# Gelu evaluated twice by ScalarE in the FFN of a fused attention + FFN block, VectorE's cast of its values removed

## The reference

```
x = x + attn(layernorm(x))     # layernorm inside attn again; gated, relu^2 linear attention,
                               # 16 heads of 32, causal running sums kv and k, then W_proj
x = x + ffn(layernorm(x))      # P = x@U1 (512->128); H = gelu_tanh(P@V1 + b1) (128->2048)
                               # Q = H@U2 (2048->128); Q@V2 + b2 (128->512)
```

## Time and profile before

| what | value |
|---|---|
| median of 3 runs | 1833.25 us (1833.06 to 1835.95) |
| the profiled execution's own time | 1834.25 us |
| its span in the trace | 1831.9 us |
| PE busy | 1792.6 us, 98% |
| PE weight loads (PEld) | 1539.9 us, 84% |
| DVE busy | 1448.5 us, 79% |
| ACT busy | 683.9 us, 37% |
| POOL busy | 798.7 us, 44% |
| granted PE clock over the span | 0.995 |
| chain that ended last, by engine | PE 93%, DVE 1% |

### The profile page before, as it was taken

How to read it: one execution, slowest core, us unless ns; L and a number is a source line. 1 busy time by engine, 2 the same in 40 slices (tenths; PEclk the granted TensorE clock), 3 DMA queues, 4 the chain that set the end, 5 groups by cost and what they waited for, 6 DMA issues and landing times.

```text
span 1831.9 us, 34348 instructions
## 1 busy us (share of the span) xinstructions
PE 1792.6 (98%) x13753; PEld 1539.9 (84%) x13753; DVE 1448.5 (79%) x2606; ACT 683.9 (37%) x1242; POOL 798.7 (44%) x1027
## 2 busy tenths in 40 slices
PE   7899999999999999999999999999999999999997
PEld 4688888888888888888888888888888888888876
DVE  7777878878878878878878788778887788787775
ACT  4233343343333333333333433333433433333332
POOL 3253444444444444435434444434444444444430
PEclk9999999999999999999999999999999999999999
DMA  6001000001010011010011010011010010100000
GB/s 216 26 13 35 29 31 31 24 29 36 24 35 24 24 36 36 24 36 25 24 36 36 24 36 24 25 35 35 25 36 24 24 36 25 35 24 27 28 18 24
DMA packets 34508, 61.06 MB, mean 33 GB/s; under 512 B 3672, under 2 KB 6256, under 8 KB 34352
## 3 DMA queue, kind: packets, MB, share of 16 engines
q1 hardware_dynamic: 33488, 57.31, 9.6%
q10 hardware_dynamic: 864, 1.57, 0.2%
HBM read 41.96 MB, written 16.91 MB: 32 GB/s over the span
## 4 chain that ended last, share of the span: by engine, by line
PE 93%; DVE 1%; POOL 0%; ACT 0%; issue 0%
PE ps_a L786 9%; PE ps_a L784 9%; PE ps_a L785 9%; PE ps_t L791 6%; PE ps_b L786 6%; PE ps_b L785 6%; PE ps_b L784 6%; PE ps_q L784 4%; PE ps_b L984 3%; PE ps_h L784 3%; PE ps_h L785 3%; PE ps_h L786 3%; PE ps_q L785 3%; PE ps_q L786 3%; PE ps_c L962 3%; PE ps_c L974 3%
## 5 line engine op out<-in xcount | busy, mean ns | idle before, releaser
L378 POOL TENSOR_TENSOR h_lo<-h_full,h_hi 128x512 fp32r<-128x512 f32 x244 | 313.8, 1286 | 500.7 <-DVE h_hi L604 500.7
L459 ACT ACTIVATE h_full<-ps_h,cols 128x256 f32<-128x256 f32 x512 | 211.1, 472 | 243.7 <-PE ps_h L786 236.0
L604 DVE CAST h_hi<-h_full 128x512 fp32r<-128x512 f32 x256 | 176.2, 688 | 98.0 <-ACT h_full L459 97.8
L784 PE MATMUL ps_b<-wx_hi,zt_hi 128*128 128x512 f32 x512 | 206.9, 404 | 5.3 <-DVE key_sums L714 3.1
L784 PE MATMUL ps_a<-wx_hi,zt_hi 128*128 128x512 f32 x512 | 208.2, 407 | 0.0
L786 PE MATMUL ps_b<-wx_hi,zt_lo 128*128 128x512 f32 x512 | 203.3, 397 | 0.0
L785 PE MATMUL ps_b<-wx_lo,zt_hi 128*128 128x512 f32 x512 | 203.2, 397 | 0.0
L786 PE MATMUL ps_a<-wx_hi,zt_lo 128*128 128x512 f32 x512 | 202.3, 395 | 0.0
L785 PE MATMUL ps_a<-wx_lo,zt_hi 128*128 128x512 f32 x512 | 201.8, 394 | 0.0
L340 POOL TENSOR_TENSOR small<-moments,eps_col 128x1 f32<-128x1 f32 x128 | 25.8, 201 | 391.5 <-DVE moments L753 327.1
L784 PE MATMUL ps_q<-h_hi,u_hi 128*128 128x256 f32 x512 | 159.5, 311 | 7.3 <-DVE h_lo L609 5.1
(11 more groups left out here) (173 smaller groups left out, 5053.0 us busy)
## 6 DMA issues: line engine op xcount, KB each, us to landing
xs<-L_attn_x SPq DMA_DIRECT2D x64, 256.0 KB, 2.8
out<-x1s SPq DMA_DIRECT2D x64, 256.0 KB, 2.1
key_sums<-carry_rows SPq DMA_DIRECT2D x60, 256.0 KB, 3.2
x1s<-L_attn_W_gate SPq DMA_DIRECT2D x4, 256.0 KB, 4.0
x1s<-L_ffn_U SPq DMA_DIRECT2D x4, 256.0 KB, 3.8
carry_rows<-key_sums SPq DMA_DIRECT2D x64, 2.0 KB
probs<-L_attn_W_qkv SPq DMA_DIRECT2D x3, 256.0 KB, 6.0
bias<-L_attn_b_qkv ACTq DMA_DIRECT2D x3, 256.0 KB, 6.8
```

The source lines that it names most:

```text
L378: E.tensor_tensor(h_lo[:, i % 2, :], h_full[:, i % 2, :], h_hi[:, i % 2, :].bitcast(F32), ALU.subtract).then_inc(s["h_lo_ready"], 1)
L459: last = E.activation(h_full[:, i % 2, a * GROUP:(a + 1) * GROUP], ps_h[i % 2][:, a * GROUP:(a + 1) * GROUP], ACT.Gelu_apprx_tanh, bias=b1 ...
L604: E.tensor_copy(h_hi[:, i % 2, :], h_full[:, i % 2, :]).then_inc(s["h_hi_ready"], 1)
L784: E.matmul(ps, wh, mh, start=start and i == 0, stop=False)
```

## The change

ScalarE evaluates gelu twice from PSUM for each half of a pair: once into `h_full` (fp32), once into `h_hi` (fp32r). Four ACTIVATEs instead of two, and only the last signals `h_full_ready`. DVE's CAST is gone; POOL's subtraction (and in the last steps DVE's) now waits for ACT. The semaphore `h_hi_ready` is gone.

```diff
             def h_tail(g, i):                                    # POOL
-                pool.wait_ge(s["h_hi_ready"], g.done(PAIRS, i + 1))
+                pool.wait_ge(s["h_full_ready"], g.done(PAIRS, i + 1))
                 E.tensor_tensor(h_lo[:, i % 2, :], h_full[:, i % 2, :], h_hi[:, i % 2, :].bitcast(F32),
                                 ALU.subtract).then_inc(s["h_lo_ready"], 1)
...
             def gelu(g, i):                                      # ACT
                 act.wait_ge(s["h_done"], g.done(PAIRS, i + 1))
-                for a in range(2):
-                    last = E.activation(h_full[:, i % 2, a * GROUP:(a + 1) * GROUP],
-                                        ps_h[i % 2][:, a * GROUP:(a + 1) * GROUP], ACT.Gelu_apprx_tanh,
-                                        bias=b1_cols[:, 2 * i + a:2 * i + a + 1])
+                for out_ in (h_full, h_hi):
+                    for a in range(2):
+                        half = slice(a * GROUP, (a + 1) * GROUP)
+                        last = E.activation(out_[:, i % 2, half], ps_h[i % 2][:, half], ACT.Gelu_apprx_tanh,
+                                            bias=b1_cols[:, 2 * i + a:2 * i + a + 1])
                 last.then_inc(s["h_full_ready"], 1)
...
-            def h_head(g, i, tail=False):                        # DVE
+            def h_tail(g, i):
                 dve.wait_ge(s["h_full_ready"], g.done(PAIRS, i + 1))
-                E.tensor_copy(h_hi[:, i % 2, :], h_full[:, i % 2, :]).then_inc(s["h_hi_ready"], 1)
-                if tail:
-                    dve.wait_ge(s["h_hi_ready"], g.done(PAIRS, i + 1))
-                    dve.wait_ge(s["h_lo_ready"], g.done(PAIRS, i))
-                    E.tensor_tensor(h_lo[:, i % 2, :], ...)
+                dve.wait_ge(s["h_lo_ready"], g.done(PAIRS, i))
+                E.tensor_tensor(h_lo[:, i % 2, :], ...)
...
-                if ffn.exists:                 # five such places: h_head in every step
-                    h_head(ffn, pairs[3], finishing)
+                if ffn.exists and finishing:   # now h_tail in the last steps alone
+                    h_tail(ffn, pairs[3])
```

More of the change, by code:

```diff
@@ L197, in block_kernel @@
             y_done x1_steps x1_small z1_ready x1b_ready tx_done x1t_hi_ready x1t_ready
-            p_done pt_hi_ready pt_ready h_done h_full_ready h_hi_ready h_lo_ready
+            p_done pt_hi_ready pt_ready h_done h_full_ready h_lo_ready
             qacc_done qt_hi_ready qt_ready result_done result_ready carry_in""".split()
@@ L600, in squared_relu @@
                     .then_inc(chain, 1)
-            def h_head(g, i, tail=False):
+            def h_tail(g, i):
                 dve.wait_ge(s["h_full_ready"], g.done(PAIRS, i + 1))
-                E.tensor_copy(h_hi[:, i % 2, :], h_full[:, i % 2, :]).then_inc(s["h_hi_ready"], 1)
-                if tail:
-                    dve.wait_ge(s["h_hi_ready"], g.done(PAIRS, i + 1))
-                    dve.wait_ge(s["h_lo_ready"], g.done(PAIRS, i))
-                    E.tensor_tensor(h_lo[:, i % 2, :], h_full[:, i % 2, :], h_hi[:, i % 2, :].bitcast(F32),
-                                    ALU.subtract).then_inc(s["h_lo_ready"], 1)
+                dve.wait_ge(s["h_lo_ready"], g.done(PAIRS, i))
+                E.tensor_tensor(h_lo[:, i % 2, :], h_full[:, i % 2, :], h_hi[:, i % 2, :].bitcast(F32),
+                                ALU.subtract).then_inc(s["h_lo_ready"], 1)
             def step(p, b):
@@ L665, in step @@
                         .then_inc(s["pt_ready"], 1)
-                if ffn.exists and b % 2 == 0:
-                    h_head(ffn, pairs[0], finishing)
+                if ffn.exists and b % 2 == 0 and finishing:
+                    h_tail(ffn, pairs[0])
                 if n.exists:
@@ L676, in step @@
                     tile_tails(early_tiles)
-                if ffn.exists:
+                if ffn.exists and finishing:
                     if b % 2:
-                        h_head(ffn, pairs[0], finishing)
-                    h_head(ffn, pairs[1], finishing)
+                        h_tail(ffn, pairs[0])
+                    h_tail(ffn, pairs[1])
                 if c.exists:
@@ L687, in step @@
                             .then_inc(s["probs_ready"], 1)
-                    if ffn.exists:
-                        h_head(ffn, pairs[2], finishing)
+                    if ffn.exists and finishing:
+                        h_tail(ffn, pairs[2])
                     dve.wait_ge(s["state_done"], c.done())
@@ L700, in step @@
                         .then_inc(s["ot_ready"], 1)
-                elif ffn.exists:
-                    h_head(ffn, pairs[2], finishing)
+                elif ffn.exists and finishing:
+                    h_tail(ffn, pairs[2])
                 z_tail(Chunk(p, b + 1))
-                if ffn.exists:
-                    h_head(ffn, pairs[3], finishing)
+                if ffn.exists and finishing:
+                    h_tail(ffn, pairs[3])
                 if n.exists:
```

## The result

The changed kernel takes **1846.05 us** (median of 4 runs, 1845.22 to 1848.57) against 1833.38 for the kernel before: ratio **1.0071, 95% interval 1.0058 to 1.0083**. It is 12.7 us slower; I had forecast 18.0 (1851). The profiled execution took 1845.22 us, 11.0 more than the profiled one of before, and the spans differ by 11.2 us. What follows explains these 11; the other 1.7 of the medians is within what single runs differ by (2.9 us between the shortest and the longest run of the kernel before).

A forecast was written before the change was run, and what follows sets the result against it. PE, busy 1648.45 of 1650 us, was taken to be bound by how late its next operand is; 16.2 (30 x 0.54) + 0.5 + 1.3 gave +18.0 us, forecast 1851.2; own range 1847 to 1856, overall range 1836 to 1857.

The forecast's parts named there:

- second rival: Odd step: L721 gets in ahead of h_lo of pair 3, q_pair 3 waits 0.25 us; 11 us slower, 1844; chance 0.08.
- h_lo starts 0.28 later: Each pair where DVE was free for the cast: gelu to POOL's subtraction takes 0.82 us instead of 0.54.
- The 0.07 more per delay: Skill page's estimate of 0.80 us for two more ACTIVATEs, not the trace's 0.73: each delay 0.07 longer, some 2 us in all.
- Odd step, front: PE 0.28 us late at q_pair 0, 0.22 won back at q_pair 2 as key_lo gets shorter: net +0.06.
- h_lo of pair 3 pushes L721, and L388 pushes L595: Odd step's end: DVE operations finding POOL's running end some 0.55 us after it, so x1t_lo comes 0.56 later.
- The two near races: POOL's h_lo of pair 3 starts before L721 (margin 0.22 us), and L388 before L595 (0.23 us).
- the first rival: L595 gets in before POOL's L388, so x1t_lo is not later: only 3.2 us slower, 1836.5; chance 0.15.
- the third, faster: Gelu's way no longer than the cast's: q_pair 0 unmoved, 0.2 us won at q_pair 2 per odd step; 1828.4; chance 0.06.
- Transposes of keys: Even step: PE's load waits for x1t_lo, 0.02 us slack at most; +0.54 us per odd and even step, 30 times.
- Last steps: Cast goes, longer gelu way delays q_pair 0, 2 and 3 and the step before: together 1.3 us.
- Last odd step: The last odd step pushes the chain that PE waits for in the tail: 0.5 us.
- Even step costs nothing; no loss of clock: Even step's delays stay within slack, over 1 us at the transposes; rival of lost clock, 1869, had chance 0.06.

The follow-up runs named there:

- e8: Kernel before, but pair 2 of odd steps alone gets two gelus and no cast: 1829.17 us, ratio 0.9973 against the kernel before.
- e3: Changed kernel with POOL's L388 also waiting until DVE's L596 is done: 1838.26 us, ratio 1.0023 against the kernel before.
- e5: Changed kernel with POOL's h_lo of pair 3 also waiting, in every step, until DVE's L718 is done: 1856.61 us, ratio 1.0122 against the kernel before.
- e1: Changed kernel, but pair 3 of each odd step keeps one gelu and DVE's cast: 1837.99 us, ratio 1.0020 against the kernel before.
- e2: Changed kernel, but pair 0 of each odd step keeps one gelu and DVE's cast: 1837.75 us, ratio 1.0022 against the kernel before.
- e7: Changed kernel, but casts kept for pairs 0 and 3 of odd steps and in the last steps: 1828.73 us, ratio 0.9971 against the kernel before.
- e4: Kernel before with POOL's L388 also waiting until DVE's L595 is done: 1834.38 us, ratio 1.0002 against the kernel before.

## Why the prediction was right, and what it mis-sized

Direction, mechanism and place were right; the sum was 18.0 where 12.7 came (11.2 in the spans). 1846.05 lies 1 us below my own range for this case (1847 to 1856), and by the time alone it is nearer to the second rival's 1844 than to my 1851.2; it is the traces, not the time, that decide between them.

- *h_lo starts 0.28 later.* 1.64 us from gelu to subtraction against 1.38: 0.26. The handover from ACT to POOL, for which no row stood, is 941.72 - (940.80 + 0.84) = 0.08; I took 0.09. The two more ACTIVATEs took 0.72 (0.73 taken). The 0.07 more per delay that I set beside this as an estimate would enter twice, as the handover's ends do: some 4 us in all, not 2.
- *Odd step, front: 0.28 lost at q_pair 0, 0.22 won at q_pair 2.* The load of q_pair 0 waits 0.49 instead of 0.23, and q_pair 2 comes 5.33 behind it instead of 5.56: 0.25 lost, 0.23 won. Right, net +0.02 for +0.06. That it was the cast of pair 2 that blocked key_lo, e8 shows.
- *h_lo of pair 3 pushes L721, and L388 pushes L595.* Both as written: 1.58 us each, ending 0.55 and 0.54 behind POOL. e3 shows the second meeting to be needed for the wait at the transposes, e5 that L718's length is POOL's doing, e1 and e2 that the 0.5 us consist of pair 3's own way and of PE's lateness at pair 0. The two near races (0.22 and 0.23 us) went as forecast, in all 30 pairs of steps. So the first rival (margin too small) fell, and the second too, as no load of q_pair 3 waits; the third, faster, is what remains if pairs 0 and 3 are left alone (e7).
- *Transposes of keys: the term that was mis-sized.* I took the lateness of the load for the lateness of PE: 0.48. The load was late by just that (19.63 against 19.15 in e3, where nothing holds it), but the next load only by 0.31 (20.02 against 19.71). In a running stream of matmuls of 512 columns a load stands 0.22 us ahead of its matmul (956.08 in the earlier trace rows; the matmul at 956.30), behind the one still running; a late load is followed by its matmul at once, 962.66 and 962.67, and some more is lost behind it:

```profile
962.19 0.40 PE L783 MATMUL ps_b<-wx_hi,zt_lo 128*128 128x512 f32 x1
962.67 0.66 PE L788 MATMUL ps_t<-ident,keys 128*128 128x128 f32 x4
963.08 0.36 PE L781 MATMUL ps_h<-pt_hi,v_hi 128*128 128x256 f32 x1
```

  So at this place the first 0.17 us of lateness are free. e1 is the small dose: load 0.23 late (19.38), next 0.06 late. I had measured the slack on the load, 0.02, and it is some 0.17 more. Per pair of steps: 0.25 - 0.23 + 0.31 = 0.33 by the parts, 0.348 by the period, where I had 0.54; x 30 = 10.4 for 16.2. That is 5.8 of the 6.8 us between the sums.
- *Last steps: 1.3.* Waits of PE for h_lo went from 5.1 to 6.2: the one of 1.41 in the earlier trace rows is 1.67 (I wrote 1.68). That is 1.1.
- *Last odd step: 0.5.* Half of it came: the wait of the transposes of queries for DVE grew from 0.48 to 0.74, those behind it stayed (1.41 and 1.42 for x1t_lo).
- *The sum of the parts.* 10.4 + 1.1 + 0.3 = 11.8. That the spans differ by nearly as much, 11.2, is in part luck. By stretches: up to the first q_pair 0 the two traces take 106.1 and 107.6 us; the 30 pairs of steps behind it differ by 10.2; the rest takes 64.5 and 64.1, though the waits above grew there by 1.4. In that last stretch the granted clock was 0.92 before and 0.97 in the changed kernel's trace (the column ahead of the last two):

```profile
1767.40:1831.00 63.60, 47.44 (x366) 41.22 (x366) 35.85 (x68) 16.26 (x37) 9.15 (x10) 0.92 0.05 17
```
```profile
1779.00:1843.00 64.00, 45.02 (x366) 39.06 (x366) 29.84 (x53) 26.75 (x67) 9.13 (x10) 0.97 0.05 17
```

  Such differences come without the change too: e4, whose pairs of steps last as long as before, takes 107.4 us up to the first q_pair 0.
- *Even step costs nothing; no loss of clock.* Right: no other wait appeared in the pairs of steps, and the granted clock of the whole span is 0.997 (0.995 before).

The lock of the shared ports (the Trainium skill, SBUF — State Buffer, SBUF: two separate sides) agrees with every run: L718 or L596 (or L721, L595), where it meets POOL's operation, ends 0.54 to 0.56 us behind it, and takes 693 or 752 ns where it does not. The 0.55 is less than these, so a part of such an operation passes while POOL's still runs. Without these meetings the forecast would have been +3.

## What to carry to other kernels

When work moves from a busy engine to an idle one, ask how long the way of each use becomes, and not for the busy shares: here 128 us less on VectorE cost 12.7, and the same edit on 31 of 256 uses, those with slack on the new way and an obstruction on the old, won 4.8. When an operation of POOL shifts by half a microsecond, follow which two-input DVE operation it now meets, and that one's chain to PE's next wait. The same goes for a mending move: L388 moved out of the way of L596 ran into the next operation on keys. And take what a wait costs PE from a later operation of its stream, compared between two runs, not from the idle time of the load.

## What the runs showed that I had not expected

How much of a late weight load PE really loses depends on the place. At the transposes of keys, behind matmuls of 512 columns, a load 0.23 late cost 0.06 and one 0.48 late cost 0.31: the 15.8 us of waits for x1t_lo stood for 0.31 x 30 = 9.3 us. At q_pair 3 of e5, behind matmuls of 512 columns too, a load 0.48 late (9.66 us behind q_pair 0's instead of 9.18 in e3) left the load of the transposes of keys 0.35 late (19.49 against 19.15). At q_pair 2, behind matmuls of 256 columns, nothing is free: the load of the kernel before is 0.23 late against the changed one (5.56 and 5.33), its matmul only 0.11, but the matmul behind that 0.22, and so is the load of q_pair 3 (9.40 and 9.18). PE there, in the kernel before and in the changed one (q_pair 0 loads at 936.68 and 943.04):

```profile
942.24 0.39 PE L784 MATMUL ps_q<-h_hi,u_hi 128*128 128x256 f32 x1
942.46 0.28 PE L785 MATMUL ps_q<-h_lo,u_hi 128*128 128x256 f32 x1
```
```profile
948.49 0.28 PE L781 MATMUL ps_q<-h_hi,u_hi 128*128 128x256 f32 x1
948.60 0.28 PE L782 MATMUL ps_q<-h_lo,u_hi 128*128 128x256 f32 x1
```

So neither the load nor the first matmul behind it tells the loss. Why the free part differs was not tested.
